# An MLP's second layer in split fp32r: three 256-column products per token tile, or one of 512 columns and one of 256

## The chip, the cores and the metric

The kernel runs on one core of one Trainium2 chip. The metric is the device time of one execution in microseconds (us). Below, PE or TensorE is the matmul engine (PEld its weight loads), DVE is VectorE, ACT is ScalarE, POOL is GpSimd, SP is SyncE, which issues most DMAs here.

## The reference

A layer norm of x, then x plus 16-head attention plus a mixture of 16 experts on the normed tokens, the latter with a residual and a layer norm of its own. The change lies in the experts. Cut to that part, with the shapes of this case (4 x 2048 tokens, D = 256, 16 experts of 64 hidden units):

```python
xn = layernorm(x)
x = x + attention(xn) + ffn(xn)

def ffn(x, wg, bg, w1, b1, w2, b2, gamma, beta):
    scores = softmax(x @ wg + bg)                 # 16 experts, the best 2 kept
    ...                                           # per expert the 1024 best tokens of each sequence
    h = einsum("ebld,edf->eblf", xg, w1) + b1
    h = gelu(h)
    out = einsum("eblf,efd->ebld", h, w2) + b2
    outs = zeros_like(x).at[b_idx, seq_ids].add(out)
    z = x + outs
    return (z - mean(z)) / sqrt(var(z) + eps) * gamma + beta
```

## The kernel before, in words

The kernel has four stages one behind the other: norm, project, attend (by far the longest) and finish. Only finish is changed. It takes the 8192 tokens in 16 blocks of 512 and doesn't gather: every expert works on every token, and a mask that is 0 or 1 for each expert and token is multiplied into gelu's output.

The 16 experts go in 8 pairs, numbered e; a pair has 2 x 64 = 128 hidden units. All products of fp32 data are made of two parts each: a value is split into an upper half (`_hi`, rounded to fp32r) and the remainder (`_lo`), and hi x hi, hi x lo and lo x hi are added up. For a block and an e:

- **hide** (TensorE, line 1180): six products of 512 columns give the hidden units `h_ps[e % 2]`, [128 units, 512 tokens]. There are two such banks.
- **gelu** (ScalarE, line 1258) reads the bank and writes `g`.
- **gate** (VectorE, line 1294) multiplies `g` by the mask. `mask_bc` comes by DMA.
- **g_hi** (ScalarE, line 1261) rounds `g`; **g_lo** (GpSimd, line 1414) is `g - g_hi`. Each of `g`, `g_hi`, `g_lo` has two buffers, by e % 2.
- **unhide** (TensorE, lines 1183 to 1193): for each of the 4 token tiles k of 128 tokens, `g_hi` or `g_lo` of the tile is the stationary operand (one weight load each time) and a 256-column row of `w2` for this e the moving one. The sum over e of all products of a tile gathers in the bank `o_ps[k]`, of which 256 of 512 columns are used.

TensorE's order is written out by hand. It runs two iterations ahead with the first layer: in iteration e of a block stand hide(e + 2), for e = 6 and 7 that of the next block, and then unhide(e). Ahead of unhide(0) also stands `project` (24 products of 256 columns, line 1213) for the block before, behind unhide(5) `hand_out` (two products that spread the attention's inverse sums, line 1200), ahead of unhide(7) `add_bias` (four products, line 1221). unhide(0) waits for `z_done`: o_ps[k] must have been read before it is written anew.

VectorE's order in a block (function `gates`) is: gate(0); gate(1), then for the block before `add_sum` (z = z + o_ps[k], four additions, line 1303) and `statistics` (lines 1308 and 1312); gate(2), then `centre` (line 1318); gate(3); gate(4), then `rebase` (line 1330), which waits for the inverse deviation `rstd`; gate(5), then `add_quotients` (line 1343); gate(6), then `divide` (line 1323), which waits for hand_out; gate(7), then `split_quotients` (line 1335). The DVE queue is strictly in this order. GpSimd makes g_lo(0), g_lo(1), then `invert` (lines 1419 and 1420: `rstd` from the statistics), then g_lo(2) to g_lo(7). ScalarE makes gelu(e) and g_hi(e) in turn, and num_hi (line 1272) behind g_hi(7).

After the last block VectorE does the z sum, the statistics, the centring, the rebase and the last additions once more, and SyncE stores the result.

`add_sum` waits tile by tile: for the first three tiles on `summed`, which the last product of tile k gives in iteration 7, and for the fourth on `used`.

Of the kernel before, what the change touches and what calls it, by code (L numbers as in the profile page):

```python
# [26 lines left out]
F32R = mybir.dt.float32r  # L27
# [6 lines left out]
P = 128  # L34
B, S, D = 4, 2048, 256
# [6 lines left out]
BLK = 512  # L42
TPB = BLK // P
# [4 lines left out]
EP = E // 2  # L48
# [56 lines left out]
def build(nc, x, wqT, wkT, wvT, woT, bq, bk, bv, bo, wg, bg, w1, b1, w2, b2, gamma, beta, out):  # L105
    top = ExitStack()
    with top:
        def sb(name, shape, dt=F32, ctx=top):
            return ctx.enter_context(nc.sbuf_tensor(name, shape, dt))
# [27 lines left out]
        with nc.sbuf_tensor("v_all", [P, B, H, ST, HD], F32) as v_all:  # L137
            pass
        w1_hi = sb("w1_hi", [P, KC, E * F], F32R)
        w2_lo = sb("w2_lo", [P, EP, D], F32R)  # L140
        w2_hi = sb("w2_hi", [P, EP, D], F32R)
        xn_hi0, xn_lo0 = (sb(f"xn_{w}0", [P, KC * BLK], F32R) for w in ("hi", "lo"))
        woT_sb = sb("woT_sb", [P, KC, D])
        wo_hi = sb("wo_hi", [P, KC, D], F32R)
# [48 lines left out]
        with ExitStack() as st:  # L193
            finish(nc, sem, lambda *a: sb(*a, ctx=st), lambda *a: ps(*a, ctx=st), locals())
# [835 lines left out]
def finish(nc, sem, sb, ps, t):  # L1030
    QTR = EP // 4
    AHEAD = 2
    w1_hi, w1_lo, w2_hi, w2_lo, woT_sb, wo_hi = (t[w] for w in ("w1_hi", "w1_lo", "w2_hi", "w2_lo", "woT_sb", "wo_hi"))
# [4 lines left out]
    b2_rows = sb("b2_rows", [PARTS * E, D], BF16)  # L1038
# [3 lines left out]
    mask_rows = sb("mask_rows", [PARTS * E, BLK], BF16)  # L1042
    x_in = sb("xe_in", [P, TPB, D])
    z = sb("z", [P, TPB, D])
# [14 lines left out]
    inv_parts = sb("inv_parts", [P, PARTS, BLK], BF16)  # L1059
    res = [sb(f"res{u}", [P, TPB, D]) for u in range(2)]  # L1060
    h_ps = [ps(f"h_ps{r}", [P, BLK]) for r in range(2)]
    o_ps = [ps(f"o_ps{k}", [P, BLK])[:, 0:D] for k in range(TPB)]
    inv_ps = ps("inv_ps", [P, KC, BLK])
    y_ps = [inv_ps[:, j, :].rearrange("p (k d) -> p k d", k=2) for j in range(2)]

# [11 lines left out]
    split = sem("e_split")  # L1077
    used = sem("e_used")
    summed = sem("e_summed")
    z_done = sem("e_z")  # L1080
    bn_done, mv_done, rstd_done, pool_chain = sem("e_bn"), sem("e_mv"), sem("e_rstd"), sem("e_pool")
    centred = sem("e_centred")
    based = sem("e_based")
# [6 lines left out]
    with nc.Block() as block:  # L1090
# [75 lines left out]
        @block.tensor  # L1166
        def _(pe):
            pe.sem_inc(used, 2)

            def hide(blk, u, e):  # L1170
                n = blk * EP + e
                if e == 0:
                    pe.wait_ge(xn_in[u], (blk // 2 + 1) * 32)
                pe.wait_ge(gelu, n + 1)
                pair = slice(e * P, (e + 1) * P)
                for c in range(KC):
                    col = slice(c * BLK, (c + 1) * BLK)
                    hi, lo = xn_hi[u][:, col], xn_lo[u][:, col]
                    for k, (w, v) in enumerate(((w1_hi[:, c, pair], hi), (w1_hi[:, c, pair], lo), (w1_lo[:, c, pair], hi))):
                        ins = pe.matmul(h_ps[e % 2][:, :], w, v, start=(c == 0 and k == 0), stop=(c == KC - 1 and k == 2))  # L1180
                ins.then_inc(hidden, 1)

            def unhide(blk, u, e):
                pe.wait_ge(split, blk * EP + e + 3)
                for k in range(TPB):
                    if e == 0:
                        pe.wait_ge(z_done, blk * TPB + k + 1)
                    hi, lo = (part[:, k * P:(k + 1) * P] for part in (g_hi[e % 2], g_lo[e % 2]))
                    for m, (v, w) in enumerate(((hi, w2_hi), (hi, w2_lo), (lo, w2_hi))):
                        ins = pe.matmul(o_ps[k], v, w[:, e, :], start=(e == 0 and m == 0), stop=(e == EP - 1 and m == 2))  # L1190
                    if e == EP - 1 and k < TPB - 1:
                        ins.then_inc(summed, 1)
                ins.then_inc(used, 1)

            def hand_out(blk):
                pe.wait_ge(spread_chain, 4)
                pe.wait_ge(num_in, (blk + 1) * 16 * NUM_LOADS)
                pe.wait_ge(added, blk * 2 + 2)
                for c in range(KC):
                    ins = pe.matmul(inv_ps[:, c, :], spread[:, c * P:(c + 1) * P], inv[:, :], start=True, stop=True)  # L1200
                ins.then_inc(spread_out, 1)

            def project(blk):
                pe.wait_ge(wo_split, 1)
                pe.wait_ge(num_split, blk + 1)
                pe.wait_ge(divided, blk + 1)
                for j in range(2):
                    for k in range(2):
                        tok = (2 * j + k) * P
                        for c in range(KC):  # L1210
                            hi, lo = (part[:, c, tok:tok + P] for part in (num_hi, num_lo))
                            for m, (v, w) in enumerate(((hi, wo_hi), (hi, wo_lo), (lo, wo_hi))):
                                ins = pe.matmul(y_ps[j][:, k, :], v, w[:, c, :],  # L1213
                                                start=(c == 0 and m == 0), stop=(c == KC - 1 and m == 2))
                    ins.then_inc(projected, 1)

            def add_bias(blk):
                pe.wait_ge(b2_placed, 16 * PARTS)
                pe.wait_ge(rows_in, (blk + 1) * 16)
                for k in range(TPB):  # L1220
                    pe.matmul(o_ps[k], mask_rows[:, k * P:(k + 1) * P], b2_rows[:, :], start=False, stop=False)  # L1221

            def block_step(blk, u, last=True, following=True):
                for e in range(EP):
                    if e + AHEAD < EP:
                        hide(blk, u, e + AHEAD)
                    elif following:
                        hide(blk + 1, 1 - u, e + AHEAD - EP)
                    if last and e == 0:
                        project(blk - 1)  # L1230
                    if e == EP - 1:
                        add_bias(blk)
                    unhide(blk, u, e)
                    if e == 5:
                        hand_out(blk)

            for e in range(AHEAD):
                hide(0, 0, e)
            block_step(0, 0, last=False)
            with pe.Fori(0, NBLK // 2 - 1) as i:  # L1240
                for u in (1, 0):
                    block_step(i * 2 + 2 - u, u)
            block_step(NBLK - 1, 1, following=False)
            project(NBLK - 1)
# [39 lines left out]
        def _(dve):  # L1284
# [11 lines left out]
            def add_sum(blk):  # L1296
                dve.wait_ge(loaded, (blk + 1) * 32)
                for k in range(TPB):
                    if k < TPB - 1:
                        dve.wait_ge(summed, blk * (TPB - 1) + k + 1)  # L1300
                    else:
                        dve.wait_ge(used, (blk + 1) * EP + 2)
                    dve.tensor_tensor(z[:, k, :], z[:, k, :], o_ps[k], ALU.add).then_inc(z_done, 1)  # L1303

            def statistics(blk):
                dve.wait_ge(z_done, blk * TPB + 2 * TPB)
# [56 lines left out]
            def gates(blk, u, last=True, following=True):  # L1363
                for e in range(EP):
                    gate(blk, e)
                    if not last and 1 <= e <= 2:
                        invert_sums(2 * e - 2)
                        invert_sums(2 * e - 1)
                    if not last and 3 <= e < 2 + PARTS:
                        split_inverses(e - 3)  # L1370
                    if not last and e == 2 + PARTS:
                        last_inverses()
                    if last and e == AHEAD - 1:
                        add_sum(blk - 1)
                        statistics(blk - 1)
                    if last and e == AHEAD:
                        centre(blk - 1)
                    if last and e == AHEAD + 2:
                        rebase(blk - 1)
                    if last and e == 5:  # L1380
                        add_quotients(blk - 1, 1 - u)
                    if e == (6 if following else EP - 1):
                        divide(blk)
                    if e == EP - 1:
                        split_quotients(blk)

            gates(0, 0, last=False)
            with dve.Fori(0, NBLK // 2 - 1) as i:
                for u in (1, 0):
                    gates(i * 2 + 2 - u, u)  # L1390
            gates(NBLK - 1, 1, following=False)
            add_sum(NBLK - 1)
            statistics(NBLK - 1)
            centre(NBLK - 1)
# [83 lines left out]
```

## Time and profile before

| | us |
|---|---|
| median of 3 runs | 3134.67 |
| lowest and highest | 3131.41, 3136.79 |
| the profiled execution's own time | 3134.84 |
| its span, first to last instruction | 3133.1 |
| busy: TensorE | 3083.6 (98%) |
| busy: VectorE | 2863.5 (91%) |
| busy: ScalarE | 2444.6 (78%) |
| busy: GpSimd | 947.8 (30%) |

The busy shares are those of the whole span, of which most is attention. The last stage begins near 2690 us; in it the engines' shares are different, so it has to be read by itself. Matmuls overlap in the records: the duration of one says less than the distance from its start to the start of the next.

### The profile page before, as it was taken

How to read it: one execution, taken by the hardware profiler on the slowest of the kernel's cores; microseconds unless marked ns; L12 is line 12 of the kernel's file. 1: busy time of each engine (PE TensorE's matmuls, PEld its weight loads, DVE VectorE, ACT ScalarE, POOL GpSimd, SP SyncE). 2: the span in 40 equal slices, each digit the busy share in tenths (PEclk: the TensorE clock that was granted, in tenths of full speed). 3: DMA queues.
4: the chain of work that ended last, by engine and by line, in shares of the span. 5: the costliest groups of instructions: out<-in, count | busy, mean ns of one | idle time of the engine just before them, and what ended most of it. 6: DMA issues, size and time to landing. Idle time of an engine off the chain costs nothing.

```text
span 3133.1 us, 73284 instructions
## 1 busy us (share of the span) xinstructions
PE 3083.6 (98%) x23912; PEld 1563.2 (50%) x23912; DVE 2863.5 (91%) x4046; ACT 2444.6 (78%) x4631; POOL 947.8 (30%) x1403
## 2 busy tenths in 40 slices
PE   7999999999999999999999999999999999999998
PEld 6544444444444444444444444444444444688887
DVE  7758999999999999999999999999999999466666
ACT  3557888888888888888888888888888888544443
POOL 2551222222222222222222222222222232344444
PEclk9999999999999999999999999999999999999999
DMA  5685333333333333333333333333433331555554
GB/s 189 199 244 102 59 59 59 59 59 59 63 63 62 61 66 64 63 59 59 59 59 59 59 59 59 64 62 64 66 63 61 59 76 39 142 161 162 164 161 127
DMA packets 139857, 271.93 MB, mean 87 GB/s; under 512 B 30144, under 2 KB 75264, under 8 KB 127296
## 3 DMA queue, kind: packets, MB, share of 16 engines
q1 hardware_dynamic: 137472, 266.71, 40.3%
q8 instruction: 199, 3.26, 0.5%
q10 hardware_dynamic: 2112, 1.35, 0.2%
q14 instruction: 74, 0.61, 0.1%
HBM read 173.59 MB, written 84.93 MB: 83 GB/s over the span
## 4 chain that ended last, share of the span: by engine, by line
PE 90%; issue 1%; DVE 0%; DMA 0%; SPq 0%; POOL 0%; ACT 0%; POOLq 0%; DVEq 0%; ACTq 0%
PE a_ps L917 35%; PE s_ps L907 35%; PE m_ps L899 8%; PE o_ps L1190 5%; PE h_ps L1180 5%; PE inv_ps L1213 1%; DMA mask_bc<-mask_b 0%; PE inv_ps L1200 0%; PE o_ps L1221 0%; POOL g_lo L1414 0%; DVE bn_z L1308 0%; DVE z L1303 0%; SPq L1097 0%; DVE num L1323 0%; ACT num_hi L1272 0%
## 5 line engine op out<-in xcount | busy, mean ns | idle before, releaser
L989 DVE TENSOR_REDUCE half_max<-m_ps 128x1 f32<-128x1024 f32 x3009 | 2370.1, 861 | 8.5 <-PE m_ps L899 8.3
L867 ACT ACTIVATE prob<-s_ps 128x512 f32<-128x512 f32 x4096 | 2123.1, 602 | 287.1 <-PE s_ps L907 287.0
L907 PE MATMUL s_ps<-q_feat,k_feat 50*128 50x512 f32 x4096 | 1438.6, 450 | 2.4 <-ACTq L859 2.4
L899 PE MATMUL m_ps<-k_feat,q_feat 48*128 48x512 f32 x4012 | 1333.3, 432 | 0.3 <-DVE half_max L989 0.3
L917 PE MATMUL a_ps<-prob,v_head 128*32 128x512 f32 x12280 | 1201.5, 463 | 3.5 <-issue 3.5
L907 PEld LDWEIGHTS s_ps<-q_feat,k_feat 50*128 50x128 f32 x4096 | 683.5, 184 | 896.9 <-ACT prob L867 849.7
L899 PEld LDWEIGHTS m_ps<-k_feat,q_feat 48*128 48x128 f32 x4012 | 650.0, 185 | 7.5 <-DVE half_max L989 1.1
L917 PEld LDWEIGHTS a_ps<-prob,v_head 128*32 128x32 f32 x12280 | 242.9, 108 | 475.2 <-issue 456.3
L711 POOL CAST shift<-row_max 128x16 fp32r<-128x16 f32 x63 | 12.3, 195 | 819.7 <-DVE row_max L975 819.7
L704 POOL COPY v_head<-v_all 128x256 f32 (+1 forms) x64 | 25.3, 397 | 757.3 <-PE a_ps L917 757.2
L1261 ACT ACTIVATE g_hi<-g 128x512 fp32r<-128x512 f32 x128 | 81.0, 633 | 214.5 <-DVE g L1294 174.1
L1414 POOL TENSOR_TENSOR g_lo<-g,g_hi 128x512 fp32r<-128x512 f32 x128 | 173.2, 1353 | 206.0 <-ACT g_hi L1261 205.8
L739 POOL TENSOR_SCALAR step_of<-route,cand 64x256 f32<-64x256 f32 x217 | 198.5, 915 | 44.5 <-POOL held L740 38.3
L1294 DVE TENSOR_TENSOR g<-g,mask_bc 128x512 f32<-128x512 f32 x128 | 108.9, 851 | 94.4 <-ACT g L1258 82.1
L740 POOL TENSOR_TENSOR held<-held,step_of 64x256 f32<-64x256 f32 x217 | 157.3, 725 | 39.8 <-POOL step_of L739 39.8
L1190 PE MATMUL o_ps<-w_hi,g_hi 128*128 128x256 f32 x512 | 146.9, 287 | 4.4 <-POOL g_lo L1414 4.4
L1190 PE MATMUL o_ps<-w_lo,g_hi 128*128 128x256 f32 x512 | 144.8, 283 | 0.0
L1190 PE MATMUL o_ps<-w_hi,g_lo 128*128 128x256 f32 x512 | 144.8, 283 | 0.0
L1258 ACT ACTIVATE g<-h_ps,b_col 128x512 f32<-128x512 f32 x128 | 87.2, 682 | 36.8 <-PE h_ps L1180 34.3
L1180 PE MATMUL h_ps<-xn_hi,w_hi 128*128 128x512 f32 x256 | 103.6, 405 | 3.0 <-ACTq L1251 3.0
L506 POOL TENSOR_TENSOR parts<-f32s,parts 128x512 fp32r<-128x512 f32 x64 | 89.0, 1396 | 57.4 <-ACT parts L487 56.9
L1190 PEld LDWEIGHTS o_ps<-w_hi,g_hi 128*128 128x128 f32 x512 | 97.4, 190 | 14.6 <-POOL g_lo L1414 7.0
(145 smaller groups left out, 2009.5 us busy)
## 6 DMA issues: line engine op xcount, KB each, us to landing
q_feat<-q_parts SPq DMA_DIRECT2D x384, 128.0 KB, 4.2
k_feat<-k_parts SPq DMA_DIRECT2D x384, 128.0 KB, 5.7
q_parts<-parts SPq DMA_DIRECT2D x32, 512.0 KB, 4.2
k_parts<-parts SPq DMA_DIRECT2D x32, 512.0 KB, 4.4
att_dram<-att SPq DMA_DIRECT2D x64, 256.0 KB, 6.3
mask_bc<-mask_b SPq DMA_DIRECT2D x128, 128.0 KB, 4.4
x_in<-in_x SPq DMA_DIRECT2D x16, 512.0 KB, 4.4
xn_dram<-xn SPq DMA_DIRECT2D x16, 512.0 KB, 5.0
```

The lines of the kernel that those rows point to most:

```text
L506: pool.tensor_tensor(parts[m][:, 1, :], f32s[m % KC][:, :], parts[m][:, 0, :].bitcast(F32), ALU.subtract).then_inc(split, 1)
L739: do(pool.tensor_scalar(step_of[:, :], t["route"][:, c * PART:(c + 1) * PART], bound, None, ALU.is_ge))
L740: do(pool.tensor_tensor(held[:, :], held[:, :], step_of[:, :], ALU.add))
L867: act.activation(prob[tile(r, kt) % R][:, cols(j)], s_ps[slot(r, kt, j) % R][:, :], ACT.Exp).then_inc(exped, 1)
L899: pe.matmul(m_ps[j // 2][:, (j % 2) * BLK:(j % 2 + 1) * BLK], q_feat[r % 2][LOW, qt * P:(qt + 1) * P], k_feat[r % 2][LOW, j * BLK:(j + 1) ...
L907: pe.matmul(s_ps[slot(r, kt, j) % R][:, :], k_feat[r % 2][UP, kt * P:(kt + 1) * P], q_feat[r % 2][UP, cols(j)], start=True, stop=True).the ...
L917: ins = pe.matmul(a_ps[qb * VW:(qb + 1) * VW, lo:hi], v_head[r % R][:, kt, :], prob[tile(r, kt) % R][:, qb * BLK + lo:qb * BLK + hi], star ...
L989: dve.tensor_reduce(half_max[r][:, qt, o:o + 1], max_source(m_ps, o), AX.X, ALU.max).then_inc(maxed, 1)
L1180: ins = pe.matmul(h_ps[e % 2][:, :], w, v, start=(c == 0 and k == 0), stop=(c == KC - 1 and k == 2))
L1190: ins = pe.matmul(o_ps[k], v, w[:, e, :], start=(e == 0 and m == 0), stop=(e == EP - 1 and m == 2))
L1294: dve.tensor_tensor(g[e % 2][:, :], g[e % 2][:, :], mask_bc[q % 2][:, e % QTR, :], ALU.mult).then_inc(gated, 1)
L1414: pool.tensor_tensor(g_lo[e % 2][:, :], g[e % 2][:, :], g_hi[e % 2][:, :].bitcast(F32), ALU.subtract).then_inc(split, 1)
```

## The change

The upper and the lower half of `w2` now lie in one tensor, `w2_both` [128, 2, 8, 256]. For each e and k, `g_hi` of the tile is loaded once, and one product of 512 columns passes both halves of w2's row e: hi x hi lands in the first half of the bank `o_ps[k]`, hi x lo in the second, which was unused. The third product, lo x hi, goes to the first half as before, with 256 columns. The bias product too goes to the first half. Both halves of a bank have to be added to z: `add_sum` first adds the four first halves and signals `z_half` for each, and then the four second halves, each of which waits for its `z_half` and signals `z_done`. The statistics and the next block's unhide(0) wait for `z_done` as before. The split of w2 into its halves writes the same two places under the new name.

```diff
-        w2_lo = sb("w2_lo", [P, EP, D], F32R)
-        w2_hi = sb("w2_hi", [P, EP, D], F32R)
+        w2_both = sb("w2_both", [P, 2, EP, D], F32R)
+        w2_lo, w2_hi = (w2_both[:, k] for k in range(2))
...
-    o_ps = [ps(f"o_ps{k}", [P, BLK])[:, 0:D] for k in range(TPB)]
+    o_ps = [ps(f"o_ps{k}", [P, 2, D]) for k in range(TPB)]
...
-    z_done = sem("e_z")
+    z_done, z_half = sem("e_z"), sem("e_z_half")
...
-                    for m, (v, w) in enumerate(((hi, w2_hi), (hi, w2_lo), (lo, w2_hi))):
-                        ins = pe.matmul(o_ps[k], v, w[:, e, :], start=(e == 0 and m == 0), stop=(e == EP - 1 and m == 2))
+                    pe.matmul(o_ps[k][:, :, :], hi, t["w2_both"][:, :, e, :], start=(e == 0), stop=False)
+                    ins = pe.matmul(o_ps[k][:, 0, :], lo, w2_hi[:, e, :], start=False, stop=(e == EP - 1))
...
-                    pe.matmul(o_ps[k], mask_rows[:, k * P:(k + 1) * P], b2_rows[:, :], start=False, stop=False)
+                    pe.matmul(o_ps[k][:, 0, :], mask_rows[:, k * P:(k + 1) * P], b2_rows[:, :], start=False, stop=False)
...
-                    dve.tensor_tensor(z[:, k, :], z[:, k, :], o_ps[k], ALU.add).then_inc(z_done, 1)
+                    dve.tensor_tensor(z[:, k, :], z[:, k, :], o_ps[k][:, 0, :], ALU.add).then_inc(z_half, 1)
+                for k in range(TPB):
+                    dve.wait_ge(z_half, blk * TPB + k + 1)
+                    dve.tensor_tensor(z[:, k, :], z[:, k, :], o_ps[k][:, 1, :], ALU.add).then_inc(z_done, 1)
```

On TensorE, the end of an unhide in the loop (its tiles k = 2 and 3) and the start of the next hide stand so before:

```order
L1190 MATMUL o_ps<-w_hi,g_hi 128x256
L1190 MATMUL o_ps<-w_lo,g_hi 128x256
L1190 MATMUL o_ps<-w_hi,g_lo 128x256
L1190 MATMUL o_ps<-w_hi,g_hi 128x256
L1190 MATMUL o_ps<-w_lo,g_hi 128x256
L1190 MATMUL o_ps<-w_hi,g_lo 128x256
L1174 REGISTER_ALU
L1180 MATMUL h_ps<-xn_hi,w_hi 128x512
L1180 MATMUL h_ps<-xn_lo,w_hi 128x512
```

And so in the changed kernel, the same two tiles and the same hide:

```order
L1189 MATMUL o_ps<-w_both,g_hi 128x512
L1190 MATMUL o_ps<-w_both,g_lo 128x256
L1189 MATMUL o_ps<-w_both,g_hi 128x512
L1190 MATMUL o_ps<-w_both,g_lo 128x256
L1174 REGISTER_ALU
L1180 MATMUL h_ps<-xn_hi,w_hi 128x512
L1180 MATMUL h_ps<-xn_lo,w_hi 128x512
```

Six products of 256 columns have become two of 512 and two of 256, and everything behind them stands as it did.

On VectorE, the rows between gate(1) and gate(2) of a block in the loop, from the third addition of the z sum on, are these before (REGISTER_ALU and ISA rows compute and wait for semaphore values):

```order
L1303 TENSOR_TENSOR z<-z,o_ps 128x256
L1302 REGISTER_ALU
L1303 TENSOR_TENSOR z<-z,o_ps 128x256
L1306 ISA
L1308 BN_STATS bn_z<-z 128x6 x4
L1312 BN_AGGR mv_z<-bn_z 128x2 x4
L1293 REGISTER_ALU
L1294 TENSOR_TENSOR g<-g,mask_bc 128x512
L1318 SCALAR_TENSOR_TENSOR z<-z,mv_z,gamma_bc 128x256 x4
```

And in the changed kernel, from the fourth addition on (line 1303 adds first halves, line 1306 second halves):

```order
L1303 TENSOR_TENSOR z<-z,o_ps 128x256
L1305 ISA
L1306 TENSOR_TENSOR z<-z,o_ps 128x256
L1305 REGISTER_ALU
L1306 TENSOR_TENSOR z<-z,o_ps 128x256
L1305 REGISTER_ALU
L1306 TENSOR_TENSOR z<-z,o_ps 128x256
L1305 REGISTER_ALU
L1306 TENSOR_TENSOR z<-z,o_ps 128x256
L1309 REGISTER_ALU
L1311 BN_STATS bn_z<-z 128x6 x4
L1315 BN_AGGR mv_z<-bn_z 128x2 x4
```

Four additions, each with a wait of its own, have come in between the z sum and the statistics; gate(2), the centring and all gates behind them stand later in the queue by that much.

## Rows read from the trace of the kernel before

**Rows 1.** The page, part 1: busy us, share of the span, instructions, by engine.

```profile
PE 3083.6 (98%) x23912; PEld 1563.2 (50%) x23912; DVE 2863.5 (91%) x4046; ACT 2444.6 (78%) x4631; POOL 947.8 (30%) x1403
```

**Rows 2.** The page, part 4: shares of the chain that ended last, by engine.

```profile
PE 90%; issue 1%; DVE 0%; DMA 0%; SPq 0%; POOL 0%; ACT 0%; POOLq 0%; DVEq 0%; ACTq 0%
```

**Rows 3.** Table of stretches: length, busy (count) by engine, clock, DMA, GB/s.

```profile
2911.63:2938.45 26.82, 26.82 (x176) 23.71 (x175) 17.79 (x33) 11.20 (x17) 12.39 (x10) 1.00 0.54 158
```

**Rows 4.** List of waits, 2804.32 to 3099.41 us: total us, times, longest us.

```profile
PEld h_ps L1180 <- issue: 4.7, 11, 0.4
```

**Rows 5.** Timeline of TensorE: start us, duration us, engine, line, operation.

```profile
2916.27 0.40 PE L1180 MATMUL h_ps<-xn_hi,w_hi 128*128 128x512 f32 x1
2916.51 0.39 PE L1180 MATMUL h_ps<-xn_lo,w_hi 128*128 128x512 f32 x1
2916.74 0.39 PE L1180 MATMUL h_ps<-xn_hi,w_lo 128*128 128x512 f32 x1
2916.96 0.28 PE L1190 MATMUL o_ps<-w_hi,g_hi 128*128 128x256 f32 x1
...
2919.78 0.28 PE L1190 MATMUL o_ps<-w_hi,g_hi 128*128 128x256 f32 x1
...
2921.22 0.40 PE L1180 MATMUL h_ps<-xn_hi,w_hi 128*128 128x512 f32 x1
...
2922.60 0.28 PE L1190 MATMUL o_ps<-w_hi,g_hi 128*128 128x256 f32 x1
```

**Rows 6.** Line 1303 over the span: ns min/median/max, first and last start.

```profile
L1303 DVE TENSOR_TENSOR z<-z,o_ps x64: 406/408/417, 2722.7 to 3122.7; 128x256 f32<-128x256 f32 x64
```

**Rows 7.** Timeline of VectorE, around one z sum; [idle before <-releaser].

```profile
2903.58 1.22 DVE L1323 TENSOR_TENSOR num<-num,inv_ps 128x1024 f32<-128x1024 f32 x1 [3.15 <-PE inv_ps L1200]
...
2910.40 1.30 DVE L1294 TENSOR_TENSOR g<-g,mask_bc 128x512 f32<-128x512 f32 x1 [1.27 <-ACT g L1258]
2911.63 1.40 DVE L1303 TENSOR_TENSOR z<-z,o_ps 128x256 f32<-128x256 f32 x4
...
2915.56 1.67 DVE L1318 SCALAR_TENSOR_TENSOR z<-z,mv_z,gamma_bc 128x256 f32<-128x256 f32 x4
2917.89 1.05 DVE L1294 TENSOR_TENSOR g<-g,mask_bc 128x512 f32<-128x512 f32 x1 [0.66 <-ACT g L1258]
2920.70 0.81 DVE L1294 TENSOR_TENSOR g<-g,mask_bc 128x512 f32<-128x512 f32 x1 [1.77 <-ACT g L1258]
2921.44 2.70 DVE L1330 SCALAR_TENSOR_TENSOR base<-z,rstd_z,xe_in 128x256 f32<-128x256 f32 x4
2924.06 0.68 DVE L1294 TENSOR_TENSOR g<-g,mask_bc 128x512 f32<-128x512 f32 x1
```

**Rows 8.** Timeline of GpSimd, the same stretch.

```profile
2909.87 1.29 POOL L1414 TENSOR_TENSOR g_lo<-g,g_hi 128x512 fp32r<-128x512 f32 x1 [2.42 <-ACT g_hi L1261]
2912.45 1.30 POOL L1414 TENSOR_TENSOR g_lo<-g,g_hi 128x512 fp32r<-128x512 f32 x1 [1.29 <-ACT g_hi L1261]
...
2916.91 1.47 POOL L1414 TENSOR_TENSOR g_lo<-g,g_hi 128x512 fp32r<-128x512 f32 x1
...
2922.26 1.59 POOL L1414 TENSOR_TENSOR g_lo<-g,g_hi 128x512 fp32r<-128x512 f32 x1 [1.29 <-ACT g_hi L1261]
2925.49 1.29 POOL L1414 TENSOR_TENSOR g_lo<-g,g_hi 128x512 fp32r<-128x512 f32 x1 [1.63 <-ACT g_hi L1261]
```

**Rows 9.** Timeline of TensorE and GpSimd in block 0: a release by g_lo.

```profile
2708.03 1.45 POOL L1414 TENSOR_TENSOR g_lo<-g,g_hi 128x512 fp32r<-128x512 f32 x1 [5.00 <-ACT g_hi L1261]
...
2709.53 0.39 PE L1190 MATMUL o_ps<-w_hi,g_hi 128*128 128x256 f32 x1 [2.23 <-POOL g_lo L1414]
2709.75 0.28 PE L1190 MATMUL o_ps<-w_lo,g_hi 128*128 128x256 f32 x1
```

**Rows 10.** Timeline of ScalarE, g_hi(2) of the block above.

```profile
2915.84 0.64 ACT L1261 ACTIVATE g_hi<-g 128x512 fp32r<-128x512 f32 x1 [2.89 <-PE o_ps L1190]
```

**Rows 11.** The chain that ended last, in order of time: start us, us, what.

```profile
3121.68 1.42 DVE z L1303 x4
```

## The prediction

> **What bounds the kernel now.** I read the page first: TensorE is busy for 98% of the span and no other engine comes near it [rows 1], and the chain of work that ended last runs through TensorE for 90% of the span [rows 2]. The change touches only the last stage, so the rest of the reading is there. The table of stretches gives the stage's beat: a block of tokens takes 26.82 us, and TensorE is busy in all of it, with the full clock granted [rows 3]. In the eleven blocks from 2804.32 to 3099.41 us the list of waits has nothing for TensorE's products, and for its weight loads only three lines of "issue", the longest sum 4.7 us in 11 times [rows 4]; none is a wait for another engine. So a block is the sum of TensorE's instructions, and I need their spacing, not their printed duration, for pipelined matmuls overlap. From the first 256-column product of one unhide (2919.78) to the first 512-column product of the next hide (2921.22) there are twelve spacings in 1.44 us, 0.12 each; from there to the next unhide (2922.60) six in 1.38 us, 0.23 each [rows 5]. One iteration e is thus 2.82 us. For its unhide it needs gelu(e) from ScalarE, gate(e) from VectorE, g_hi(e) from ScalarE and g_lo(e) from GpSimd, in this order. The numbers e below are those of the block in which the z sum of the block before stands at 2911.63; its unhides 2 and 3 start at 2919.78 and 2922.60.
>
> **What the change removes.** In each of 16 x 8 x 4 = 512 pairs (e, k), three spacings of 0.12 (0.36) become one of 512 columns and one of 256: 0.23 + 0.12 = 0.35. That is 0.01 us a pair, 0.04 an unhide, 0.32 a block. The columns are the same, 768; only one weight load and one instruction's overhead go. The ends: neighbouring 512-column products stand 0.24 or 0.23 apart, and the step from the last of them to a 256-column product is 0.22 [rows 5], so a pair lies between 0.34 (gain 0.64 a block) and 0.36 (gain nothing). No row shows a 512-column operand that is read as two pieces 8 KB apart, as here; the nearest is the contiguous one, and I give no extra for the gap but keep 0.01 a pair (a loss of 0.32 a block) as the far end. I take 0.35, since it is the mean of many spacings.
>
> The Trainium skill, page "TensorE: Matmul & The Clock Gate", section "Back-to-back issue gap", gives N / 2.4 + 2.5 ns, which makes a pair 327.5 ns before and 325 ns after: by that page an estimate of 1.2 us over 15 blocks, a quarter of what the rows give. The trace's spacings are wider than the page's (0.12 us against 109 ns, 0.23 against 216 ns), so I go by the trace.
>
> **What it adds.** Four more additions on VectorE in each block. The four of today take 1.40 us together [rows 7], 406 to 417 ns each by record [rows 6]; four more are 1.33 (spaced as they are now) to 1.64 (one after the other), and I take 1.40. The last of today's run while GpSimd works on g_lo from 2912.45 [rows 8] and take no longer for it, so I add nothing for that.
>
> The Trainium skill, page "SBUF — State Buffer", section "Who interferes with whom", says why: a VectorE instruction with one SBUF source (the other here is PSUM) keeps clear of GpSimd, one with two waits for it. The trace agrees on both: the additions keep to 406 to 417 ns, the gates don't keep to theirs (below).
>
> First cover: unhide(0) waits for each bank's last addition. It starts at 2919.78 - 2 x 2.82 = 2914.14 now, and 0.08 earlier with the two unhides ahead of it shortened. The second addition of bank 0 ends at 2911.63 + 1.40 + 0.41 = 2913.44, that of bank 3 near 2914.44, and they are needed at 2914.06 and 2915.1. This is covered, with 0.6 to spare.
>
> Second cover, and it fails: what is queued behind the additions. On VectorE these are the statistics, gate(2), the centring, gate(3), gate(4), the rebase and gate(5) [rows 7]; on GpSimd the inverse deviation, which waits for the statistics, and g_lo(2) right behind it at 2916.91 [rows 8]. Up to there everything moves by 1.40.
> - g_lo(2) starts at 2918.31 and takes 1.47 as now, so it ends at 2919.78. A released weight load follows g_lo's end by 0.05 (2708.03 + 1.45, then 2709.53), and behind such a start the next product comes after 0.22 instead of 0.12, so 0.10 more is lost [rows 9]. TensorE, four unhides shortened, would be there at 2919.62. It loses 2919.78 + 0.05 + 0.10 - 2919.62 = 0.31 us.
> - gate(2) is done near 2917.0 (the centring now starts behind it at 2915.56), g_hi(2) follows where it now starts at 2915.84 [rows 10], and the centring runs until 2915.56 + 1.67 + 1.40 = 2918.63. gate(3) behind it meets g_lo(2) and is held: the gate at 2910.40 started 0.53 into a g_lo (2909.87, 1.29) and ended 0.54 after that one's end [rows 7, 8]. So gate(3) ends at 2920.32 (now 2918.94), g_hi(3) runs from 2920.35 and g_lo(3) from 2921.05 to 2922.35. TensorE wants it at 2922.7: no further wait.
> - gate(4) is again held, by g_lo(3), to 2922.89; the rebase starts at 2922.83, against 2921.44 now, still 1.39 late. gate(5) and g_lo(5) keep that, and g_lo(5), now 2925.49 to 2926.78, ends at 2928.17. With 0.05 and 0.10 as above unhide(5) has its effective start at 2928.32. Now it is 2922.60 + 5.64 = 2928.24.
>
> So at e = 5 VectorE's line sets the time, 0.08 later than today, and what TensorE saved up to there (seven unhides, 0.28) is gone. After it only unhide(5)'s own 0.04 is kept. Then comes hand_out, before which VectorE stands idle for 3.15 us until TensorE releases its division, as now [rows 7]; that restores the order, and the next z sum hangs on that hand_out. Per block: +0.08 - 0.04 = +0.04, in 15 blocks +0.6 us. In block 0 there is no z sum, and TensorE waits for g_lo there now (2.23 us at 2709.53 [rows 9]), so I count no gain in it.
>
> **The end.** In the last block the z sum stands in the chain to the store and is covered by nothing [rows 11]. Four more additions: +1.4 us (1.33 to 1.64).
>
> **Sum.** The profiled execution took 3134.84 us, 1.7 of it outside its span of 3133.1, and lies 0.17 over the median of 3134.67. 3134.84 + 0.6 + 1.4 = 3136.8 us. A measurement of this kernel can tell 0.2% from no change: under 3128.4, or over 3140.9.
>
> **Rivals.**
> - *VectorE's delay is absorbed* (14%). For it: VectorE is idle for 0.66 us ahead of gate(3) and 1.77 ahead of gate(4) [rows 7], more than the 1.40 added. Against it: both idle times end on gelu, and gelu(e+1) stands behind g_hi(e) on ScalarE, so the delay passes through them. Then the gain stays whole: 15 x 0.32 = 4.8 less and 1.4 more, 3131.4; with 0.34 a pair 9.6 less, 3126.6.
> - *It is slower* (19%). The place is unhide(5) again. g_lo takes up to 1.59 where a rebase runs beside it (2922.26 [rows 8]), against the 1.29 that I give g_lo(5), and one more gate may be held for 0.3. With both, 0.6 later: 15 x 0.64 = 9.6 and 1.4 more, 3145.8. It decides from 0.31 a block up, which is 0.27 later than I have it. Against it, the rebase is over before g_lo(5) starts in the order as I have it.
> - *The wide operand is slow* (5%). If its two pieces cost a 512-column product 0.03 more (0.26), a pair takes 0.38: 32 x 0.02 = 0.64 a block, 3145.8 as well. Nothing in the trace speaks for it.
> - *A pair costs what it cost* (within the forecast): 0.24 + 0.12. Then TensorE is at 2928.24 and waits for 0.08 only: 15 x 0.08 and 1.4 more, 3137.4. That both come out alike makes the forecast firm: at e = 5 the time is VectorE's.
>
> **How the numbers follow.** The forecast has 62%. Of the first rival's 14, 6 lie under 3128.4, the rest inside the band; of the second's 19, 5 lie inside; the third's 5 lie above. Faster 0.06, same 0.75, slower 0.19. The range goes from a little under the first rival's 3131.4 to near the slow cases, 3130 to 3145; outside stay the first rival with 0.34 a pair and the far half of the slow ones, less than 2 in 10.
>
> **What would show it.** In the changed profile: 512-column products of the second layer 0.23 ahead of their neighbour and pairs of 0.35 (wrong if over 0.36). A beat of 26.86, with waits of TensorE or its weight loads for g_lo once or twice a block, about 0.3 us, and none at e = 0 for z. g_lo(5) ends 16.5 us behind the start of the z sum. Eight additions in 2.8 us. The tail, from the last block's first z addition to the end, 1.4 longer. A beat near 26.5 without waits for g_lo proves the first rival, one over 27.14 the second.

## The result

| | before | changed |
|---|---|---|
| median | 3134.58 us (9 runs) | 3144.34 us (9 runs) |
| lowest and highest | 3131.41, 3138.90 | 3141.71, 3147.23 |
| profiled execution, its span | 3134.84, 3133.1 | 3144.34, 3142.6 |

The ratio is 1.0031, with a 95% interval from 1.0021 to 1.0042. The changed kernel is slower by 9.8 us, by more than the 0.2% that the prediction took as its bound. It lies inside the stated range of 3130 to 3145 us, 0.7 below its upper end, but in the case to which the prediction gave 19%. One of the twelve runs of one kernel below (the kernel before with two steps moved) took 4894 us at a granted clock of 0.76; it is left out of that kernel's ratio.

The profile of the changed kernel, first the table of stretches over the eleven blocks of steady state (columns as in [rows 3]):

```profile
2806.80:3107.14 300.34, 294.96 (x1565) 240.43 (x1564) 206.15 (x398) 121.84 (x187) 142.21 (x110) 1.00 0.55 156
```

300.34 / 11 = 27.30 us a block. The kernel before has 26.83 (295.09 us for the eleven from 2804.32 to 3099.41). Fifteen blocks have a z sum in them, so this is 15 x 0.477 = 7.2 us. The list of waits of the same stretch shows whom TensorE waits for, where [rows 4] had only "issue":

```profile
PEld o_ps L1189 <- POOL g_lo L1417: 10.1, 11, 0.9
...
PE o_ps L1189 <- POOL g_lo L1417: 5.4, 11, 0.5
PEld h_ps L1180 <- issue: 4.7, 11, 0.4
```

Eleven waits for g_lo, one a block. The timelines of one block show which. VectorE:

```profile
2916.02 1.40 DVE L1303 TENSOR_TENSOR z<-z,o_ps 128x256 f32<-128x256 f32 x4
2917.35 1.40 DVE L1306 TENSOR_TENSOR z<-z,o_ps 128x256 f32<-128x256 f32 x4
2918.78 1.41 DVE L1311 BATCH_NORM_STATS2 bn_z<-z 128x6 f32<-128x256 f32 x4
2920.34 0.38 DVE L1315 BATCH_NORM_AGGREGATE mv_z<-bn_z 128x2 f32<-128x6 f32 x4
2920.63 0.66 DVE L1294 TENSOR_TENSOR g<-g,mask_bc 128x512 f32<-128x512 f32 x1
2921.21 1.67 DVE L1321 SCALAR_TENSOR_TENSOR z<-z,mv_z,gamma_bc 128x256 f32<-128x256 f32 x4
2922.79 0.69 DVE L1294 TENSOR_TENSOR g<-g,mask_bc 128x512 f32<-128x512 f32 x1
2925.43 0.98 DVE L1294 TENSOR_TENSOR g<-g,mask_bc 128x512 f32<-128x512 f32 x1 [1.96 <-ACT g L1258]
```

Then, from the timelines of GpSimd, ScalarE and TensorE, the same block:

```profile
2921.46 1.12 POOL L1423 TENSOR_TENSOR rstd_z<-var_z,minus_half 128x4 f32<-128x4 f32 x1
2922.56 2.06 POOL L1417 TENSOR_TENSOR g_lo<-g,g_hi 128x512 fp32r<-128x512 f32 x1
```

```profile
2921.32 0.63 ACT L1261 ACTIVATE g_hi<-g 128x512 fp32r<-128x512 f32 x1 [3.98 <-DVE g L1294]
2921.86 0.67 ACT L1258 ACTIVATE g<-h_ps,b_col 128x512 f32<-128x512 f32 x1
```

```profile
2923.80 0.39 PE L1180 MATMUL h_ps<-xn_hi,w_lo 128*128 128x512 f32 x1
2924.67 0.50 PE L1189 MATMUL o_ps<-w_both,g_hi 128*128 128x512 f32 x1 [0.49 <-POOL g_lo L1417]
2925.01 0.28 PE L1190 MATMUL o_ps<-w_both,g_lo 128*128 128x256 f32 x1
2925.13 0.39 PE L1189 MATMUL o_ps<-w_both,g_hi 128*128 128x512 f32 x1
2925.36 0.28 PE L1190 MATMUL o_ps<-w_both,g_lo 128*128 128x256 f32 x1
```

The eight additions take 2.73 us (2916.02 to 2918.75), the statistics follow, and g_lo(2) is free to start 6.54 us behind the start of the z sum, against 5.28 in [rows 7, 8]. But it takes 2.06 us where it took 1.47. TensorE issues the last product of hide(4) at 2923.80 and would go on at 2924.03; it goes on at 2924.67, when g_lo(2) has ended at 2924.62, and behind this start the next product stands 0.34 away instead of 0.23. That is 0.64 + 0.11 = 0.75 us lost in the block (the expectations below have it as 0.74). The pairs themselves gained: behind the restart the 512-column product (2925.13 to 2925.36) takes 0.23 and the 256-column one ahead of it (2925.01 to 2925.13) 0.12.

The z sum of the last block, in the chain of work that ended last:

```profile
3129.86 1.41 DVE z L1303 x4
3131.27 1.34 DVE z L1306 x4
```

From the start of the last z sum to the end of the span are 12.74 us, 11.42 before [rows 11]: 1.3 more. 7.2 and 1.3 make 8.5 of the 9.5 us between the two spans. The remaining 1.0 lies ahead of the first z sum (2724.56 against 2722.67 us, part of it taken back in the two blocks behind it); in the kernels below that point lies anywhere from 2720.7 to 2725.1, without a relation to what was edited that I can see, so I count it as scatter.

### The profile page after: what moved, and what is told of

Read it like the earlier page. It is cut to its first block, busy times and chain, and to the rows that moved or that the text cites. A ratio compares the mean times of both kernels' runs of the same rounds, so it can differ in the third digit from the quotient of the medians.

```text
span 3142.6 us, 72380 instructions
## 1 busy us (share of the span) xinstructions
PE 3085.4 (98%) x23400; PEld 1531.7 (49%) x23400; DVE 2880.6 (92%) x4110; ACT 2443.2 (78%) x4631; POOL 956.8 (30%) x1403
## 4 chain that ended last, share of the span: by engine, by line
PE 82%; DVE 3%; issue 3%; POOL 2%; ACT 1%; DMA 0%; SPq 0%; DVEq 0%; ACTq 0%; POOLq 0%
PE a_ps L917 35%; PE s_ps L907 35%; PE m_ps L899 8%; PE h_ps L1180 2%; PE o_ps L1189 2%; POOL g_lo L1417 1%; PE o_ps L1190 1%; DVE bn_z L1311 1%; DVE g L1294 1%; DVE z L1306 1%; ACT num_hi L1272 1%; DVE z L1303 0%; ACT g L1258 0%; DMA mask_bc<-mask_b 0%; PE inv_ps L1200 0%
## 5 line engine op out<-in xcount | busy, mean ns | idle before, releaser
L1417 POOL TENSOR_TENSOR g_lo<-g,g_hi 128x512 fp32r<-128x512 f32 x128 | 181.3, 1421 | 184.6 <-ACT g_hi L1261 184.5
L1189 PE MATMUL o_ps<-w_both,g_hi 128*128 128x512 f32 x512 | 189.2, 404 | 10.8 <-POOL g_lo L1417 10.8
L1190 PE MATMUL o_ps<-w_both,g_lo 128*128 128x256 f32 x512 | 143.3, 280 | 0.0
L1189 PEld LDWEIGHTS o_ps<-w_both,g_hi 128*128 128x128 f32 x512 | 96.1, 188 | 43.2 <-POOL g_lo L1417 19.1
L1180 PE MATMUL h_ps<-xn_lo,w_hi 128*128 128x512 f32 x256 | 101.2, 395 | 0.0
```

The lines of the kernel that those rows point to most:

```text
L1189: pe.matmul(o_ps[k][:, :, :], hi, t["w2_both"][:, :, e, :], start=(e == 0), stop=False)
L1190: ins = pe.matmul(o_ps[k][:, 0, :], lo, w2_hi[:, e, :], start=False, stop=(e == EP - 1))
L1417: pool.tensor_tensor(g_lo[e % 2][:, :], g[e % 2][:, :], g_hi[e % 2][:, :].bitcast(F32), ALU.subtract).then_inc(split, 1)
```

## The experiments

Theory A: the wide product gains what it should on TensorE, and the loss comes from the four additions, over g_lo(2). Theory B: the wide operand itself costs time. Under A two things are to be told apart: A1, that g_lo(2)'s length counts (VectorE's centring and gate(3) take the port that it needs), and A2, that only its late start counts. Ratios are against the kernel before, run in the same rounds.

| kernel | median us, of before | ratio (95%) | beat | tail |
|---|---|---|---|---|
| before | 3134.58 | 1 | 26.83 | 11.42 |
| changed | 3144.34, 3134.58 | 1.0031 (1.0021 to 1.0042) | 27.30 | 12.74 |
| wide product only | 3132.51, 3136.38 | 0.9989 (0.9979 to 0.9998) | 26.55 | 11.41 |
| additions only | 3145.20, 3136.38 | 1.0031 (1.0019 to 1.0042) | 27.43 | 12.74 |
| centring later | 3143.15, 3136.38 | 1.0023 (1.0012 to 1.0034) | 27.13 | 12.74 |
| deviation later | 3139.42, 3136.38 | 1.0009 (1.0000 to 1.0019) | 26.83 | 12.75 |
| two additions | 3131.41, 3135.92 | 0.9987 (0.9978 to 0.9996) | 26.55 | 12.07 |
| gate first | 3132.29, 3135.92 | 0.9991 (0.9982 to 1.0000) | 26.55 | 12.73 |
| gate first, narrow end | 3132.15, 3135.92 | 0.9989 (0.9981 to 0.9998) | 26.55 | 11.53 |
| before, gate first | 3134.93, 3135.92 | 0.9998 (0.9989 to 1.0007) | 26.83 | 11.41 |
| three additions | 3138.85, 3137.05 | 1.0008 (0.9999 to 1.0018) | 26.99 | 12.41 |
| gate(3) behind g_lo(2) | 3141.01, 3137.05 | 1.0012 (1.0002 to 1.0022) | 27.01 | 12.74 |

The beat is that of the eleven steady blocks, the tail goes from the start of the last z sum to the end of the span; both are from the profiles.

### The wide product without the additions

```diff
-                for k in range(TPB):
-                    dve.wait_ge(z_half, blk * TPB + k + 1)
-                    dve.tensor_tensor(z[:, k, :], z[:, k, :], o_ps[k][:, 1, :], ALU.add).then_inc(z_done, 1)
```

(and the first addition signals `z_done`.)

> The wide product alone: the four additions of the second halves are left out, so the hi x lo part of the second layer is missing from the output; VectorE's queue is that of before. Theory A (TensorE gains 0.27 us a block, and the loss comes from VectorE's additions through g_lo(2)): no wait of TensorE for g_lo, a beat of 26.55 us against 26.83, 3130 us, 4 to 5 below before. Theory B (the 512-column operand in two pieces costs TensorE time that the spacings hide): a beat of 26.83 or more, 3134 us or above.

The table of stretches of this kernel over its eleven steady blocks:

```profile
2805.02:3097.03 292.01, 292.01 (x1565) 241.29 (x1564) 199.84 (x354) 123.13 (x187) 136.35 (x110) 1.00 0.56 161
```

292.01 / 11 = 26.55, as theory A has it, and TensorE waits for no other engine. The gain of the wide product is 26.83 - 26.55 = 0.28 us a block, 0.009 a pair. Theory B falls.

### The additions without the wide product

```diff
-                    dve.tensor_tensor(z[:, k, :], z[:, k, :], o_ps[k], ALU.add).then_inc(z_done, 1)
+                    dve.tensor_tensor(z[:, k, :], z[:, k, :], o_ps[k], ALU.add).then_inc(z_half, 1)
+                for k in range(TPB):
+                    dve.wait_ge(z_half, blk * TPB + k + 1)
+                    dve.tensor_tensor(z[:, k, :], z[:, k, :], o_ps[k], ALU.add).then_inc(z_done, 1)
```

> The additions alone: three narrow products as before, and each bank is added to z twice (the output counts the experts' sum twice). Theory A: g_lo(2) lasts about 2.07 us again and holds unhide(2); TensorE is 0.13 us later there than in the changed kernel, so it stands for 0.6; beat 27.4, tail 1.3 longer, 3144 to 3146 us, as slow as the changed kernel. Theory B: a beat near 26.9 and only the tail's 1.3 us, 3136.

Timeline of GpSimd, g_lo(2) of the block whose z sum starts at 2943.13:

```profile
2949.66 2.06 POOL L1417 TENSOR_TENSOR g_lo<-g,g_hi 128x512 fp32r<-128x512 f32 x1
```

g_lo(2) lasts 2.06 us here too, the beat is 27.43, and the ratio is that of the changed kernel. The whole loss is in the additions. With TensorE 0.28 a block slower the loss is 0.60 in place of 0.75, and the result 0.13 worse a block: what TensorE gains ahead of a wait for another engine shortens nothing and makes the wait longer; only what it gains behind it counts. Here that is unhides 2 to 5, about 4 x 0.035 = 0.14: in both kernels the next z sum starts 8.69 us behind hand_out, which follows unhide(5).

### The centring behind gate(3)

```diff
-                    if last and e == AHEAD:
+                    if last and e == AHEAD + 1:
                         centre(blk - 1)
```

> The changed kernel with the centring moved behind gate(3) on VectorE. Theory A1 (g_lo(2) is late by 1.4 and is then stretched from 1.47 to 2.07 us by the centring and gate(3), and it is the stretch that costs): g_lo(2) takes 1.3 to 1.5 us, TensorE's wait falls from 0.74 to 0.1 or nothing, beat 26.6 to 26.7, 3134 to 3136 us. Theory A2 (the delay of 1.4 us alone does it): g_lo(2) starts as late and the wait stays above 0.5, beat 27.2 or more, 3143 us or above.

Timelines of GpSimd and VectorE in the block from 2914.67, and the list of waits of eleven blocks:

```profile
2921.12 1.29 POOL L1417 TENSOR_TENSOR g_lo<-g,g_hi 128x512 fp32r<-128x512 f32 x1
```

```profile
2921.21 1.75 DVE L1294 TENSOR_TENSOR g<-g,mask_bc 128x512 f32<-128x512 f32 x1 [1.28 <-ACT g L1258]
```

```profile
PEld o_ps L1189 <- POOL g_lo L1417: 11.4, 33, 0.6
...
PE o_ps L1189 <- POOL g_lo L1417: 1.0, 6, 0.2
```

g_lo(2) starts 6.45 behind the z sum's start, nearly as late as in the changed kernel, takes 1.29 and now holds gate(3) instead (1.75 us), and unhide(2) no longer waits: for this place theory A1 is right. But the beat is 27.13 and not 26.7, and the time is 3143 us, which was A2's. The waits are now 33, three a block: the gates, held and then followed by the centring, make the g_lo of later iterations late (unhide(4) waits longest, 0.31 to 0.34 us, and then the next product comes 0.11 late). My expectation left this out.

### The deviation behind g_lo(2)

```diff
-                    if last and e == AHEAD - 1:
+                    if last and e == AHEAD:
                         invert(blk - 1)
```

> The changed kernel with the inverse deviation moved behind g_lo(2) on GpSimd. g_lo(2) then starts behind g_hi(2), some 5.95 us after the start of the z sum instead of 6.54, and overlaps the centring earlier. Theories A1 and A2 both: the wait at unhide(2) falls to 0.1 or nothing (the end comes 0.6 earlier if the stretch stays, more if it shrinks), beat 26.6 to 26.7, 3133 to 3136 us. If instead unhide(5), as in my prediction, becomes the next to wait, the beat is 26.8 to 26.9 and the time 3137.

The beat is 26.83, as in the last sentence of the expectation: unhide(2) doesn't wait, and the delay comes out at the later unhides. From the list of waits:

```profile
PEld o_ps L1189 <- POOL g_lo L1417: 8.5, 33, 0.3
```

Three short waits a block (at most 0.3 us of the weight load), at unhides 3 to 5, which eat the 0.28 that TensorE gained. The median is 3.0 us above that of the kernel before (3139.42, where I had 3137); 1.3 of it is the tail, and the rest is inside the interval.

### Two additions, and three

With two, for tiles 0 and 1 only:

```diff
-                    dve.tensor_tensor(z[:, k, :], z[:, k, :], o_ps[k][:, 0, :], ALU.add).then_inc(z_half, 1)
-                for k in range(TPB):
-                    dve.wait_ge(z_half, blk * TPB + k + 1)
-                    dve.tensor_tensor(z[:, k, :], z[:, k, :], o_ps[k][:, 1, :], ALU.add).then_inc(z_done, 1)
+                    dve.tensor_tensor(z[:, k, :], z[:, k, :], o_ps[k][:, 0, :], ALU.add).then_inc(z_half if k < 2 else z_done, 1)
+                    if k == 1:
+                        for i in range(2):
+                            dve.wait_ge(z_half, blk * 2 + i + 1)
+                            dve.tensor_tensor(z[:, i, :], z[:, i, :], o_ps[i][:, 1, :], ALU.add).then_inc(z_done, 1)
```

> Half the added work: second halves are added for token tiles 0 and 1 only (hi x lo is missing for tiles 2 and 3). Theory A1 (delay, and g_lo(2) stretched by VectorE's centring and gate(3) beside it): g_lo(2) starts 5.87 us behind the start of the z sum and takes between 1.47 (as before) and 2.07 us, so it ends at 7.4 to 7.9 against TensorE's 7.8: beat 26.55 to 26.85, 3131 to 3136 us. If every addition costs the same share of the loss (a quarter of 0.75 us a block each), the beat is 26.93 and the time 3139.

With three the same edit has `k < 3`, `k == 2`, `range(3)` and `blk * 3`. It was made after the result of the one with two:

> Three of the four second halves are added (hi x lo is missing for tile 3). With two the beat was 26.55, with four 27.30. g_lo(2) can start 6.21 us behind the start of the z sum. Theory A1 (it is the port: gelu(3) ends, and gate(3) can go, 0.03 us before g_lo(2) can, as with four additions and unlike with two, where gelu(3) ended 0.23 after it): g_lo(2) takes 2.06 us, ends at 8.27, and TensorE waits for about 0.4: beat 26.95 to 27.0. Theory A2 (delay alone): g_lo(2) takes 1.47, ends at 7.68, no wait, beat 26.55.

GpSimd, ScalarE and VectorE with two additions, the block whose z sum starts at 2937.61:

```profile
2943.48 1.46 POOL L1418 TENSOR_TENSOR g_lo<-g,g_hi 128x512 fp32r<-128x512 f32 x1
```

```profile
2943.02 0.69 ACT L1258 ACTIVATE g<-h_ps,b_col 128x512 f32<-128x512 f32 x1
```

```profile
2942.13 1.67 DVE L1322 SCALAR_TENSOR_TENSOR z<-z,mv_z,gamma_bc 128x256 f32<-128x256 f32 x4
2943.74 1.75 DVE L1294 TENSOR_TENSOR g<-g,mask_bc 128x512 f32<-128x512 f32 x1
```

And with three, the block from 2939.10:

```profile
2945.31 2.07 POOL L1418 TENSOR_TENSOR g_lo<-g,g_hi 128x512 fp32r<-128x512 f32 x1
```

```profile
2944.61 0.67 ACT L1258 ACTIVATE g<-h_ps,b_col 128x512 f32<-128x512 f32 x1
```

```profile
2945.55 0.68 DVE L1294 TENSOR_TENSOR g<-g,mask_bc 128x512 f32<-128x512 f32 x1
```

Two additions cost nothing in the beat (26.55), three cost 0.44 a block (26.99), four 0.75. So the price isn't one of so much an addition, and the step from two to three is g_lo(2)'s length. With two, gelu(3) ends 0.23 us after g_lo(2) has started, gate(3) comes too late, is held (1.75 us), and g_lo(2) takes 1.46. The centring ends at 2943.80, 0.09 after gelu(3), so it isn't an idle gap of VectorE that lets g_lo(2) in: gelu(3) is done before the centring is, and g_lo(2) still goes first. With three, gelu(3) ends 0.03 before g_lo(2)'s start, gate(3) goes right behind the centring (0.68 us), and g_lo(2) takes 2.07. This was theory A1's forecast, 26.95 to 27.0; the rival's was 26.55.

### gate(3) made to wait for g_lo(2)

```diff
                 dve.wait_ge(gelu, blk * EP + e + 3)
+                if e == 3:
+                    dve.wait_ge(split, blk * EP + e + 2)
```

> The changed kernel, complete, with one wait more: gate(3) waits on VectorE until g_lo(2) is done. Theory A1: g_lo(2) starts at 6.54 as in the changed kernel but takes 1.47 instead of 2.06, ends at 8.0, and TensorE's wait at unhide(2) falls from 0.74 to about 0.15: beat 26.7, or up to 26.9 where a later unhide waits for the delayed gates; 3133 to 3138 us. If the length of g_lo(2) has nothing to do with gate(3), it stays at 2.06, and the beat rises over 27.3.

Timeline of GpSimd in the block from 2942.54, and the list of waits of eleven blocks:

```profile
2949.08 1.47 POOL L1419 TENSOR_TENSOR g_lo<-g,g_hi 128x512 fp32r<-128x512 f32 x1
```

```profile
PEld o_ps L1189 <- POOL g_lo L1419: 11.8, 44, 0.3
```

GpSimd's g_lo(5) and TensorE's start of unhide(5), in the block from 2915.54:

```profile
2930.90 1.30 POOL L1419 TENSOR_TENSOR g_lo<-g,g_hi 128x512 fp32r<-128x512 f32 x1 [1.63 <-ACT g_hi L1261]
...
2932.25 0.50 PE L1189 MATMUL o_ps<-w_both,g_hi 128*128 128x512 f32 x1
2932.59 0.28 PE L1190 MATMUL o_ps<-w_both,g_lo 128*128 128x256 f32 x1
```

g_lo(2) is back at 1.47 with all four additions, by nothing but gate(3) standing aside: its length was gate(3)'s doing, and 0.6 us of the loss at unhide(2) with it. The beat falls only to 27.01, over the top of what I expected (26.9), and so is the median, 3141.01 for 3133 to 3138: gate(3), (4) and (5) are then later and four unhides a block wait a little (44 in eleven blocks). The last of them sets the block's time: unhide(5) starts 16.71 us behind the z sum's start, right behind g_lo(5), and its second product comes 0.11 late, where the kernel with the wide product alone starts it at 16.36. That is 0.46 us, all that this block loses against 26.55. This kernel is, by accident, close to what my prediction supposed of the changed one.

### Out of the way: gate(2) first

```diff
                     if last and e == AHEAD - 1:
                         add_sum(blk - 1)
+                    if last and e == AHEAD:
                         statistics(blk - 1)
```

on VectorE (where gate(2) stands between the two now), and the edit of "the deviation behind g_lo(2)" on GpSimd. The "narrow end" kernel also keeps, in the last block, the three narrow products and one z sum:

```diff
+                    if narrow:
+                        for w2 in (w2_hi, w2_lo):
+                            pe.matmul(o_ps[k][:, 0, :], hi, w2[:, e, :], start=(e == 0 and w2 is w2_hi), stop=False)
+                    else:
+                        pe.matmul(o_ps[k][:, :, :], hi, t["w2_both"][:, :, e, :], start=(e == 0), stop=False)
...
-                for k in range(TPB):
+                for k in range(0 if narrow else TPB):
                     dve.wait_ge(z_half, blk * TPB + k + 1)
```

The control is the kernel before with the two steps moved in the same way.

> The changed kernel, complete, with two steps moved: gate(2) ahead of the statistics on VectorE, and the inverse deviation behind g_lo(2) on GpSimd. Theory A: no iteration waits for g_lo any more, every addition is covered, beat 26.55 as with the wide product alone; over that kernel only the tail's 1.3 us: 0.9 to 1.0 below the kernel before times 3 us, that is a ratio of 0.999 to 0.9995. If the additions cost something wherever they stand (the rival), the beat stays at 26.8 or more and the ratio at 1.001 or above.

For the narrow end:

> As the gate-first kernel, and the last block keeps the three narrow products and a single z sum, so that nothing is added in the tail. Theory A: beat 26.55, tail 11.4 us as before, 1.3 us less than the gate-first kernel: ratio 0.9985 to 0.999. The best version that the experiments so far point to.

For the control:

> A control: the kernel before with the same two steps moved. Theory A: TensorE sets the beat there, nothing changes, 26.83 and a ratio of 1.000 within the interval. If the order by itself is worth something, the gate-first kernels owe their time to it and not to the wide product: then the beat is under 26.8.

The tables of stretches of the gate-first kernel and of the control, each over its eleven steady blocks:

```profile
2801.24:3093.26 292.02, 292.02 (x1565) 241.28 (x1564) 220.56 (x398) 118.01 (x187) 133.33 (x110) 1.00 0.57 161
```

```profile
2802.19:3097.29 295.10, 295.10 (x1916) 260.67 (x1916) 218.17 (x354) 118.85 (x187) 134.41 (x110) 1.00 0.56 159
```

292.02 / 11 = 26.55: the full gain of the wide product, with all eight additions in. g_lo(2) now starts 4.8 us behind the start of the z sum and no unhide waits. The control stays at 26.83 and 0.9998, so it is not the order by itself. Of the two moved steps, the deviation alone gave 26.83; gate(2) alone was not run. The narrow end takes the tail from 12.73 to 11.53; that is 1.2 us, too little for the two medians (3132.29 and 3132.15) to show. Both kernels are about 0.1% below the one before, the narrow end clear of 1 by its interval (0.9981 to 0.9998), the other up to its edge. They beat the changed kernel by 0.4%, and the kernel before by no more than can just be told.

## Why the prediction was right or wrong

**What bounds the kernel:** right. TensorE before, and the sum of its spacings.

**The gain on TensorE:** right in kind, a little large: 0.32 us a block said, 0.28 measured (0.009 a pair instead of 0.010). The formula of the Trainium skill (page "TensorE: Matmul & The Clock Gate", section "Back-to-back issue gap"), which that section gives for an isolated product, makes it, as an estimate, 2.5 ns a pair and 0.08 us a block; the runs show 9 ns and 0.28.

**The cost of the additions:** 1.40 said; 1.33 by the timeline, and 1.32 in the tail, where 1.4 was said. They don't suffer from GpSimd, as said: eight take 2.73 us.

**First cover, unhide(0):** right, no wait for z anywhere.

**Second cover: here a step failed.** "g_lo(2) starts at 2918.31 and takes 1.47 as now" and "gate(3) behind it meets g_lo(2) and is held". The start was right (6.68 us behind the z sum's start said, 6.54 measured). Its length was not: 2.06. I moved the centring and g_lo(2) by the same amount and kept their overlap, but didn't ask who else had become ready in the meantime. Before, gate(3) had to wait for gelu(3) until 2917.89, 0.98 us after the start of g_lo(2) [rows 7, 8]. g_lo(2) then moved by 1.26 us and gelu(3) by only 0.29 (its end lies 6.22 us behind the z sum's start before, 6.51 in the changed kernel), so that gelu(3) was done 0.03 us ahead of g_lo(2)'s start and gate(3) went first. So TensorE lost 0.75 at unhide(2), where I had 0.31. The experiments with two, three and four additions and the one that only holds gate(3) back show this cause.

**The place at unhide(5):** not reached in the changed kernel. As gate(3) wasn't held, VectorE's line was ahead again by e = 4. It exists, though, and works as I had it. In the three kernels in which gate(3) ends 8.29 us or more behind the z sum's start (centring later, deviation later, gate(3) behind g_lo(2); it is 7.45 in the changed kernel) unhides 2 to 5 or 3 to 5 wait, and the last wait swallows the others. g_lo(5) ends there 16.48 (deviation later), 16.66 (gate(3) behind g_lo(2)) and 16.78 us (centring later) behind the z sum's start, unhide(5) starts 0.05 behind that, and with the late second product (0.11) it is 0.28, 0.46 and 0.58 behind the 16.36 of the kernel with the wide product alone: just what these blocks lose. Against the kernel before, the one in which gate(3) stands aside has +0.18, where I had +0.04. 0.12 of the difference is g_lo(5), which ends at 16.66 and not at 16.54: gate(3), which there waits for g_lo(2)'s signal, ends 0.80 us behind g_lo(2), and not 0.54 as one that is held at the port.

**The next z sum:** right, it hangs on hand_out, 8.69 us behind it in the kernel before and in the changed one.

**The sum:** +0.04 a block said, +0.477 measured, 15 x 0.44 = 6.6 us of the 7.5 between forecast and median. The size of one term, TensorE's wait for g_lo, was wrong, and that decided it, since forecast and bound were 4.1 us apart. That the median still lies inside the stated range is luck: the range reached up to 3145 for the sake of slow cases at unhide(5) and of a slow operand, neither of which occurred.

**The rivals:** the slower one came true in its size (0.31 a block was its point of decision), not in its place: it was "one more gate held" that I feared, and it was one gate not held. The absorbed delay, 3131.4, is about what two additions or the reordered kernel give (3131.41 and 3132.29, in rounds in which the kernel before took 3135.92). But VectorE's line doesn't absorb the delay there, it only stays short of TensorE: g_lo(5) ends 15.73 and 16.02 us behind the z sum's start (15.15 before), and unhide(5) starts at 16.36. The wide operand isn't slow.

## What to carry to other kernels

An edit that puts work into the queue of an engine that isn't the bottleneck has to be followed down that queue until it meets one that is: here 1.33 us of additions, all covered where they stand, came out some 5 us later as a wait of TensorE, through the statistics, the inverse deviation and g_lo(2) on GpSimd. Slack has an edge: two additions were free in the beat, the third cost 0.44 us a block. And at a shared port, when steps shift by different amounts (here g_lo(2) by 1.26 us, gelu(3) by 0.29), ask anew who is ready first. The repair is to let the step that feeds the bottleneck (gate(2), g_lo(2)) go ahead of work that nothing waits for soon.

## What the runs showed of the hardware

**Who gets the port.** VectorE's instructions with two sources in SBUF (gates, centring, rebase) and g_lo on GpSimd exclude each other, as the Trainium skill says on the page "SBUF — State Buffer", in the section "Who interferes with whom": whichever is first has it, for the whole instruction, and the other blocks. The runs agree on the blocking: a gate that comes under a running g_lo ends 0.55 us behind that g_lo. What "first" means they show for gate(3) alone. When gelu(3) ended 0.03 us ahead of g_lo(2)'s start, gate(3) went first and made g_lo(2) 2.06 us long (0.92 us until VectorE's line ended at 7.46 behind the z sum's start, and 1.14 of its own); when it ended 0.23 us behind that start, gate(3) was held to 1.75 us. To stand ready in VectorE's queue is not enough, though. In every kernel here, g_lo(4) starts 0.03 to 0.05 us behind the start of the rebase's third instruction, and the fourth, which waits for nothing of its own, is held to 1.51 us (four in 2.70 us in [rows 7], where the centring's four take 1.67). With the centring or the deviation later the fourth centring instruction is held in the same way, and in the control one is held although the instruction ahead of it had started 0.24 to 0.27 us before g_lo(2). Why gate(3) gets past g_lo and these don't is open.

**A restart costs.** Where a start had to wait for g_lo and came 0.05 us behind g_lo's end, TensorE's next product came 0.11 us later than in a stream (0.34 instead of 0.23 at 512 columns, 0.22 instead of 0.11 at 256). Where g_lo had ended 0.08 to 0.14 us ahead of the start, it was 0.02 to 0.08 us. Only the restart behind the last wait of a block counts; those before it are swallowed like the waits themselves. The same 0.11 us also stand behind add_bias, at unhide(7), where nothing is waited for: in the kernel before the product after unhide(7)'s first comes after 0.22 us.
